# Windowed attention on one core: the values product per head in quarters of the array, and the outputs turned and sent through DRAM

## Chip, cores and metric

One core of a Trainium2 chip (trn2) runs the whole program in one launch. The metric is the time on the device in microseconds, the median of the runs; lower is better. TensorE is called PE in the rows, its weight loads PEld, VectorE DVE, ScalarE ACT, GpSimd POOL, and SyncE, which issues the DMAs, SP.

## What is computed

A macaron block over a tensor of 8 sequences x 512 tokens x 128 features: a mixture of experts, a Mamba layer, the mixture again, a second kind of mixture (top 1 of 8 experts plus a shared one), windowed attention, and that second mixture again, each added to its input. The change touches the attention alone:

```python
H, WIN, d, C = 16, 64, 8, 64              # 16 heads of 8 features
qkv = (x @ Wqkv.T + bqkv).reshape(B, S, 3, H, d).transpose(2, 0, 3, 1, 4)
...
scores = einsum('bhncd,bhnld->bhncl', qc, kb) / sqrt(d)
band = (j >= c) & (j < c + WIN)           # each query sees 64 keys around it
attn = softmax(where(band, scores, -inf))
o = einsum('bhncl,bhnld->bhncd', attn, vb).reshape(B, H, S, d)
return o.transpose(0, 2, 1, 3).reshape(B, S, D) @ Wout.T + bout
```

## The kernel before

**Units.** The attention works in 64 units. Sequence `s` has 4 groups of 4 heads, and each group two halves; unit `u` is `where(u)`: sequence `u // 8`, group `u % 8 // 2`, half `u % 2`. A unit holds 8 blocks of 32 queries; a block has its 4 heads x 32 queries on the 128 partitions and the 96 keys around it along the row. Each engine runs its own written-out loop over steps `t`, with `k = t % 8`, and semaphores tie them.

**One step of TensorE** (`pe`): the scores of unit t + 2 (`scores`, L1424, 8 matmuls of 128 x 96), the transposes of unit t (`turn`, L1450), the values product of unit t - 1 (`weigh`, L1469), and the fold of unit t - 2 (`gather`, L1491). Between them `PLACES` sets pieces of the next sequence's projections (T, q, k, v) and the output projection (op) of the last one: T at k = 0, q and k at k = 1, op at k = 2, v at k = 3; a piece of place 0 stands before the transposes, one of place 2 after the product.

**The values product** multiplies the turned probabilities of all 4 heads (96 keys x 128 rows) with 32 columns of values and 32 columns of ones, from the tile `vb`. So each row gets the values of all 4 heads of the group, of which only its own 8 columns are wanted, and its sum of probabilities. `normalize` on VectorE (L1476, L1480) divides, `keep_own` on GpSimd (L1362) multiplies with the mask `own` that leaves each head its columns, and `gather` multiplies with `fold`, four identities of 32 on top of each other. That adds the heads up, turns them, and puts them on the partitions of their group in the bank `BZ`, a quarter of the array per group. When all 8 units of a sequence are there, ScalarE copies the bank to `oT` (L1404), TensorE projects it (L1397) and VectorE adds it to `x` (L1409).

**Others.** VectorE: `mask` (scale and band, L1433), `find_max` (L1438), `set_keys` (rounds the keys of a group, L1282). GpSimd: `less_max` (subtracts the row maximum, L1355), `norm_root`, `bias_out`. ScalarE: `exps` (L1442), `copy_p` (L1457), `set_queries` (L1272, four casts of 32x512 that lay the queries of a group on a block diagonal). VectorE writes the keys and ScalarE the queries of group `t // 2 + 2` at the end of each even step t; they serve the units t + 4 and t + 5. SyncE stores the projected queries and keys to DRAM and loads them in strips per group, and does the same with the values.

**Waits.** An engine works off its own instructions in order; a wait holds all that stands behind it. `scores` of the first half of a group waits for both casts:

```python
if half == 0 and c == 0:
    eng.wait_ge(q_set.sem, q_set.at(n))
    eng.wait_ge(k_set.sem, k_set.at(n))
```

Of the kernel before, what the change touches and what calls it, by code (L numbers as in the profile page):

```python
# [7 lines left out]
F32 = mybir.dt.float32  # L8
# [176 lines left out]
def ffn0_up(nc, S, sb, w, cleared):  # L185
# [4 lines left out]
    W["raw_ld"] = [S.dma(f"f0_raw{r}_loaded", 2) for r in range(4)]  # L190
# [728 lines left out]
def front(nc, S, C, bank, lasting, xin, a, f0, K, w1, sorted_rows):  # L919
# [13 lines left out]
    with ExitStack() as ctx, ExitStack() as scan_ctx:  # L933
# [45 lines left out]
        raw_ld, split = [S.dma(f"k_raw{r}_loaded", (E + 1) * NU // 2) for r in range(4)], K["split"]  # L979
# [92 lines left out]
def attention(nc, S, C, bank, K, a, host):  # L1072
# [9 lines left out]
    RQ = 3  # L1082
    NG = NSEQ * HG
    scale = float(1.0 / np.sqrt(np.float32(HD)))
    with ExitStack() as ctx:
# [12 lines left out]
        band, own, fold = sb("band", [P, KW]), sb("own", [P, GD]), sb("fold", [P, QB])  # L1098
# [5 lines left out]
        v_rows = nc.dram_tensor("v_rows", [NSEQ * SEQ, D], F32, kind="Internal").ap()  # L1104

# [3 lines left out]
        tri = S.count("a_masks", 1, ("band", "own", "fold") + tuple(f"{n}{r}" for n in ("ge", "le", "own", "fold") for r in range(HG)))  # L1109
# [7 lines left out]
        q_set, k_set = S.count("a_queries_set", NG), S.count("a_keys_set", NG)  # L1117
        v_in = [S.dma(f"a_values{p}_in", NSEQ // 2, ("low", "mid", "high")) for p in range(2)]
        bz_zero = S.count("a_bz_zeroed")
        sc_done, sm_done, max_done, sub_done = S.count("a_scores_done", NU * 2), S.count("a_masked", NU * 2), S.count("a_max_done", NU), S.count("a_less_max", NU)  # L1120
        exp_done, turned, pT_done = S.count("a_exp_done", NU), S.count("a_p_turned", NU * 2), S.count("a_p_copied", NU * 2)
        pv_done, on_done, own_done = S.count("a_pv_done", NU * 2), S.count("a_out_dve", NU, ("rc", "on")), S.count("a_own_kept", NU)
        ot_done = S.count("a_fold_done", NU)
        oc_done, op_done, r_done, ob_done = S.count("a_oT_copied", NSEQ), S.count("a_proj_done", NSEQ), S.count("a_row_done", NSEQ), S.count("a_bias_added", NSEQ)
# [27 lines left out]
        def set_masks(eng):  # L1152
            eng.memset(band[:], 0.0).then_inc(tri.sem)
            eng.memset(own[:], 0.0).then_inc(tri.sem)
            eng.memset(fold[:], 0.0).then_inc(tri.sem)
            quarter = [slice(32 * r, 32 * r + 32) for r in range(HG)]
            for r, p in enumerate(quarter):
                eng.wait_ge(tri.sem, tri.at(0, f"ge{r - 1}" if r else "fold"))
                eng.affine_select(out=band[p, :], in_=band[p, :], compare_op=ALU.is_ge, fill=-1e30, base=0, pattern=[[1, KW]], channel_multiplier=-1).then_inc(tri.sem)
# [3 lines left out]
            for r, p in enumerate(quarter):  # L1163
                eng.wait_ge(tri.sem, tri.at(0, f"own{r - 1}" if r else "le3"))
                eng.memset(own[p, HD * r:HD * r + HD], 1.0).then_inc(tri.sem)
            for r, p in enumerate(quarter):
                eng.wait_ge(tri.sem, tri.at(0, f"fold{r - 1}" if r else "own3"))
                eng.affine_select(out=fold[p, :], in_=fold[p, :], compare_op=ALU.not_equal, fill=1.0, base=0, pattern=[[-1, QB]], channel_multiplier=1).then_inc(tri.sem)
            eng.wait_ge(tri.sem, tri.at(0, "fold3"))
# [83 lines left out]
        def strips(eng, s, g):  # L1253
# [4 lines left out]
            if n >= 2:  # L1258
                eng.wait_ge(q_set.sem, q_set.at(n - 2))
                eng.wait_ge(k_set.sem, k_set.at(n - 2))  # L1260
# [3 lines left out]
        def set_queries(eng, n, heads=range(HG)):  # L1264
# [64 lines left out]
        o1, oT = two("o1", [P, UB, GD]), sb("oT", [P, SEQ])  # L1329

        def sync(eng):
            for s in range(NSEQ):
                if s >= 1:
                    store_queries(eng, s)
                    store_keys(eng, s)
                    strips(eng, s, 0)
                    strips(eng, s, 1)
                    store_values(eng, s)
                eng.wait_ge(v_out.sem, v_out.at(s))
                if s <= 1:  # L1340
                    eng.wait_ge(zeroed.sem, zeroed.at(0, "vb"))
                else:
                    eng.wait_ge(pv_done.sem, pv_done.at(2 * (GU * (s - 1)) - 1))
                v, low, mid, high = vb[s % 2], slice(0, PAD), slice(PAD, PAD + QB), slice(PAD + QB, KW)
                rows = v_rows[s * SEQ:(s + 1) * SEQ, :].rearrange("(b i) d -> i b d", i=QB)
                eng.dma_start(v[low, 1:NB, :], rows[:, 0:NB - 1, :]).then_inc(v_in[s % 2].sem, 16)
                eng.dma_start(v[mid, 0:NB, :], rows).then_inc(v_in[s % 2].sem, 16)
                eng.dma_start(v[high, 0:NB - 1, :], rows[:, 1:NB, :]).then_inc(v_in[s % 2].sem, 16)
                strips(eng, s, 2)
                strips(eng, s, 3)  # L1350
# [6 lines left out]
        def keep_own(eng, u):  # L1357
            Z = o1[u % 2]
            if u == 0:
                eng.wait_ge(tri.sem, tri.at(0, "fold3"))  # L1360
            eng.wait_ge(on_done.sem, on_done.at(u, "on"))
            eng.tensor_tensor(Z[:], Z[:], own[:, None, :].to_broadcast([P, UB, GD]), ALU.mult).then_inc(own_done.sem)  # L1362

        def pool(eng):
            clear_group(eng, 1)
            for p in range(2):
# [6 lines left out]
            less_max(eng, 1)  # L1373
            for t in range(NU + 1):
                s, k = t // GU, t % GU
                if t + 2 < NU:
                    less_max(eng, t + 2)
# [902 lines left out]
```

## Time and profile before

| | |
|---|---|
| Time, median of 3 runs | 1867.86 us (1866.92 to 1868.22) |
| Profiled execution: span from first to last instruction | 1918.1 us |
| Profiled execution: a time of its own beside the span | none given; the span is 50.2 us above the median |
| Granted TensorE clock, mean | 0.971 |
| Busy: TensorE, VectorE, ScalarE, GpSimd | 1729.9, 1279.6, 1105.3, 1210.5 us |

The span is that of one execution under the profiler, and all start times and durations in the rows are from it. The time is measured without it. Busy time of an engine is the time in which it had an instruction running, so a TensorE that is busy need not be at its peak. The granted clock is in shares of 2.4 GHz; 0.50 is 1.2 GHz. A matmul on 32-bit floats appears as two records of weight load and two of matmul, one on rounded ones as one.

### The profile page before, as it was taken

How to read it: one execution, taken by the hardware profiler on the slowest of the kernel's cores; microseconds unless marked ns; L12 is line 12 of the kernel's file. 1: busy time of each engine (PE TensorE's matmuls, PEld its weight loads, DVE VectorE, ACT ScalarE, POOL GpSimd, SP SyncE). 2: the span in 40 equal slices, each digit the busy share in tenths (PEclk: the TensorE clock that was granted, in tenths of full speed). 3: DMA queues.
4: the chain of work that ended last, by engine and by line, in shares of the span. 5: the costliest groups of instructions: out<-in, count | busy, mean ns of one | idle time of the engine just before them, and what ended most of it. 6: DMA issues, size and time to landing. Idle time of an engine off the chain costs nothing. (4 is left out here: it accounts for less than half of the span.)

```text
span 1918.1 us, 35727 instructions
## 1 busy us (share of the span) xinstructions
PE 1729.9 (90%) x12089; PEld 1502.7 (78%) x12089; DVE 1279.6 (67%) x2981; ACT 1105.3 (58%) x1953; POOL 1210.5 (63%) x1201
## 2 busy tenths in 40 slices
PE   7998998999999899976779988899899999988889
PEld 6887776778878688765668867777899999877777
DVE  2358988888888987889894355334576766554333
ACT  3476766667676576756655452433677777542332
POOL 4248787787868778798985243565455555444554
PEclk9999999999999999998989999999899999989999
DMA  5023433323333233232224110113544554001113
GB/s 147 1 85 104 114 100 101 95 94 105 96 110 97 86 104 108 98 89 84 94 61 118 32 37 29 45 43 104 159 130 120 148 157 124 2 33 33 42 43 104
DMA packets 121486, 166.74 MB, mean 87 GB/s; under 512 B 14710, under 2 KB 56732, under 8 KB 121308
## 3 DMA queue, kind: packets, MB, share of 16 engines
q1 hardware_dynamic: 114268, 148.86, 25.7%
q0 software_dynamic: 7040, 15.60, 2.6%
q8 instruction: 101, 1.65, 0.4%
q14 instruction: 77, 0.63, 0.1%
HBM read 114.20 MB, written 50.20 MB: 86 GB/s over the span
## 5 line engine op out<-in xcount | busy, mean ns | idle before, releaser
L833 POOL TENSOR_TENSOR db<-du_m,bt 128x512 f32<-128x512 f32 x256 | 329.3, 1288 | 116.7 <-DVE bank L838 115.9
L838 DVE TENSOR_TENSOR_SCAN bank<-bank,db 128x512 f32<-128x512 f32 x256 | 312.6, 1221 | 18.2 <-ACT bank L823 17.7
L864 POOL TENSOR_TENSOR y_m<-y_m,ph 128x512 f32<-128x512 f32 x240 | 312.8, 1303 | 2.0 <-DVE ph L853 2.0
L823 ACT ACTIVATE bank<-dt_m,a_neg 128x512 f32<-128x512 f32 x256 | 176.3, 689 | 85.7 <-DVE ph L853 78.9
L853 DVE TENSOR_TENSOR ph<-bank,ct 128x512 f32<-128x512 f32 x240 | 165.9, 691 | 9.4 <-POOL y_m L864 1.1
L1355 POOL TENSOR_TENSOR s_a<-s_a,mx_a 128x768 f32<-128x768 f32 x64 | 94.1, 1470 | 87.1 <-DVE mx_a L1438 87.0
L1469 PE MATMUL bank<-vb_a,pT_a 96*128 96x64 f32 x1024 | 121.7, 272 | 0.0
L1469 PEld LDWEIGHTS bank<-vb_a,pT_a 96*128 96x128 f32 x1024 | 119.8, 193 | 0.0
L375 PEld LDWEIGHTS bank<-dn,hf1b 128*128 128x128 f32 x680 | 90.2, 194 | 16.1 <-DVE x_all L437 6.8
L375 PEld LDWEIGHTS bank<-dn,hf2b 128*128 128x128 f32 x680 | 90.2, 195 | 16.0 <-DVE x_all L437 8.3
L375 PEld LDWEIGHTS bank<-dn,hf0b 128*128 128x128 f32 x688 | 90.4, 193 | 12.0 <-DVE x_all L437 2.8
L375 PEld LDWEIGHTS bank<-dn,hf0a 128*128 128x128 f32 x688 | 91.6, 194 | 8.8 <-DVE x_all L437 1.2
L375 PE MATMUL bank<-dn,hf1b 128*128 128x128 f32 x680 | 91.7, 279 | 7.0 <-DVE x_all L437 5.0
L375 PE MATMUL bank<-dn,hf2b 128*128 128x128 f32 x680 | 91.8, 279 | 6.5 <-DVE x_all L437 6.1
L375 PEld LDWEIGHTS bank<-dn,hf2a 128*128 128x128 f32 x680 | 90.9, 195 | 7.6 <-DVE x_all L437 0.2
L375 PEld LDWEIGHTS bank<-dn,hf1a 128*128 128x128 f32 x680 | 89.8, 193 | 8.0 <-DVE x_all L437 0.6
L375 PE MATMUL bank<-dn,hf0b 128*128 128x128 f32 x688 | 91.9, 277 | 2.9 <-issue 1.5
L375 PE MATMUL bank<-dn,hf0a 128*128 128x128 f32 x688 | 91.8, 277 | 0.7 <-DVE x_all L437 0.7
L375 PE MATMUL bank<-dn,hf2a 128*128 128x128 f32 x680 | 91.5, 279 | 0.0
L375 PE MATMUL bank<-dn,hf1a 128*128 128x128 f32 x680 | 90.4, 276 | 0.1
L1457 ACT COPY pT_a<-bank 96x512 f32<-96x512 f32 x128 | 67.8, 580 | 32.2 <-PE bank L1450 32.2
L123 PE MATMUL bank<-xT_hi0b,up_hi 128*128 128x512 f32 x128 | 70.3, 549 | 17.5 <-ACT hf2b L406 9.3
(480 smaller groups left out, 4877.1 us busy)
## 6 DMA issues: line engine op xcount, KB each, us to landing
bt<-bc_rows SPq DMA_DIRECT2D x128, 256.0 KB, 3.4
ct<-bc_rows SPq DMA_DIRECT2D x128, 256.0 KB, 3.4
sorted<-zero_row SPq DMA_DIRECT2D x64, 288.0 KB, 4.0
k_strips_a<-k_rows SPq DMA_DIRECT2D x32, 256.0 KB, 3.0
q_strips_a<-q_rows SPq DMA_DIRECT2D x32, 256.0 KB, 4.0
q_rows<-q_hi_a SPq DMA_DIRECT2D x16, 256.0 KB, 3.0
q_rows<-q_lo_a SPq DMA_DIRECT2D x16, 256.0 KB, 3.3
k_rows<-k_hi_a SPq DMA_DIRECT2D x16, 256.0 KB, 3.2
```

Source lines behind the costliest of these rows:

```text
L123: eng.matmul(out, ahi, bhi, start=True, stop=False)
L375: x = eng.matmul(Y.psum[:, t], hf[r][:, t], W["dn"][:, e, c, :], start=c == 0 and k == 0, stop=c == HC - 1 and k == NT - 1, skip_group_che ...
L823: eng.activation(DH[J % 2][:], dt[s % 2][:, j % NH, :], ACT.Exp, scale=a_neg[:, j % NH, j // NH:j // NH + 1]).then_inc(da_done.sem)
L833: eng.tensor_tensor(db[J % RD][:], du[s % 2][:, j % NH, :], bt[N % RB][:], ALU.mult).then_inc(db_done.sem)
L838: eng.tensor_tensor_scan(DH[J % 2][:], DH[J % 2][:], db[J % RD][:], 0.0, ALU.mult, ALU.add).then_inc(hs_done.sem)
L853: eng.tensor_tensor(out, DH[J % 2][:], ct[N % RB][:], ALU.mult).then_inc(ph_done.sem)
L864: eng.tensor_tensor(y[s % 2][:, j % NH, :], y[s % 2][:, j % NH, :], ph[J % RP][:], ALU.add).then_inc(ys_done.sem)
L1355: eng.tensor_tensor(X[:], X[:], M[:, :, None].to_broadcast([P, UB, KW]), ALU.subtract).then_inc(sub_done.sem)
L1457: eng.copy(pT[u % 2][:, c * BB:(c + 1) * BB, :].rearrange("p b q -> p (b q)"), BT[c][0:KW, :]).then_inc(pT_done.sem)
L1469: x = eng.matmul(BO[:, at:at + 2 * GD], pT[u % 2][:, c * BB + j, :], vb[s % 2][:, b:NB + 1:NB - b, g * GD:(g + 1) * GD], start=True, stop= ...
```

## The change

`weigh` does a product of its own for each head: 32 columns of the turned probabilities stand in the quarter of the array that writes the head's 32 partitions, and 8 columns of its own values and 8 of ones move through. So the mask `own`, `keep_own`, `fold` and `gather` go. `normalize` writes 64 elements per partition instead of 256, in an order by feature and block. `turn_out` turns the whole unit with one transpose, ScalarE copies it from the bank (`copy_out`), SyncE stores it by columns in `o_rows` in DRAM (`store_out`), in runs of 32 floats, and loads the sequence as `oT` (`load_out`) for the output projection, which moves to k = 5.

With that come: scores and all before the exponential run 3 units ahead instead of 2 (`AHEAD`); two of the four query casts of each group (`set_queries` with heads 2 and 3) go to GpSimd, behind `less_max(t + 3)`, with a semaphore `q_set2` of their own that `scores` also waits for; the DMAs of SyncE have a new order; the norm of the finished sequence moves from k = 4 and 7 to k = 6, 7 and 0; before the last projection stand 20 filling matmuls instead of 4. The casts of keys and queries stay at the end of even steps.

```diff
+    AHEAD, RZ = 3, 4
+        o_rows = nc.dram_tensor("o_rows", [NSEQ, 2, HEADS, HD, UB, QB], F32, kind="Internal").ap()
...
-        def set_queries(eng, n, heads=range(HG)):
+        def set_queries(eng, copy, n, heads):
...
-                x = eng.copy(qd[n % RQ][p, :, r, :], q_strips[n % 2][p, :].rearrange("p (b q) -> p b q", q=QB))
-            if HG - 1 in heads:
-                x.then_inc(q_set.sem)
+                dst, src = qd[n % RQ][p, :, r, :], q_strips[n % 2][p, :].rearrange("p (b q) -> p b q", q=QB)
+                x = copy(dst, src)
+            x.then_inc(q_set.sem if 0 in heads else q_set2.sem)
...
+        def store_out(eng, u):
+            s, g, half = where(u)
+            eng.wait_ge(zc_done.sem, zc_done.at(u))
+            eng.dma_start(o_rows[s, half, g * HG:(g + 1) * HG, :, :, :].rearrange("r d b q -> (d b) r q"), zt[u % RZ][:]).then_inc(o_out[u % RZ].sem, 16)
+
+        def load_out(eng, s):
+            if s >= 1:
+                eng.wait_ge(op_done.sem, op_done.at(s - 1))
+            for r in range(RZ):
+                eng.wait_ge(o_out[r].sem, o_out[r].at((s + 1) * GU // RZ - 1))
+            eng.dma_start(oT[:], o_rows[s].rearrange("f h d b q -> (h d) f (b q)")).then_inc(oT_ld.sem, 16)
...
         def pool(eng):
             clear_group(eng, 1)
+            set_queries(eng, eng.tensor_copy, 1, (2, 3))
+            eng.wait_ge(q_set2.sem, q_set2.at(1))
...
-                if t + 2 < NU:
-                    less_max(eng, t + 2)
-                if t >= 1:
-                    keep_own(eng, t - 1)
+                if t + AHEAD < NU:
+                    less_max(eng, t + AHEAD)
+                if t % 2 == 0 and t + 4 < 2 * NG:
+                    eng.wait_ge(sub_done.sem, sub_done.at(t + AHEAD))
+                    set_queries(eng, eng.tensor_copy, t // 2 + 2, (2, 3))
+                    eng.wait_ge(q_set2.sem, q_set2.at(t // 2 + 2))
...
                 eng.wait_ge(q_set.sem, q_set.at(n))
+                eng.wait_ge(q_set2.sem, q_set2.at(n))
                 eng.wait_ge(k_set.sem, k_set.at(n))
...
-                b, at = half * UB + c * BB + j, (c * BB + j) * 2 * GD
-                x = eng.matmul(BO[:, at:at + 2 * GD], pT[u % 2][:, c * BB + j, :], vb[s % 2][:, b:NB + 1:NB - b, g * GD:(g + 1) * GD], start=True, stop=True)
+                b, at = half * UB + c * BB + j, (c * BB + j) * 2 * HD
+                for r in range(HG):
+                    p, h = slice(32 * r, 32 * r + 32), g * HG + r
+                    x = eng.matmul(BO[p, at:at + 2 * HD], pT[u % 2][:, c * BB + j, p], vb[s % 2][:, b:NB + 1:NB - b, h * HD:(h + 1) * HD], start=True, stop=True)
...
-        def gather(eng, u):
...
+        def turn_out(eng, u):
+            if u >= 1:
+                eng.wait_ge(zc_done.sem, zc_done.at(u - 1))
+            eng.wait_ge(on_done.sem, on_done.at(u, "on"))
+            eng.transpose(BZ[0:HD * UB, 0:P], o1[u % 2][:].rearrange("p d b -> p (d b)"), C["ident"][:]).then_inc(ot_done.sem)
+
+        def copy_out(eng, u):
+            if u >= RZ:
+                eng.wait_ge(o_out[u % RZ].sem, o_out[u % RZ].at(u // RZ - 1))
+            eng.wait_ge(ot_done.sem, ot_done.at(u))
+            eng.copy(zt[u % RZ][:], BZ[0:HD * UB, 0:P]).then_inc(zc_done.sem)
 
         def pe(eng):
-            for u in range(2):
+            for u in range(AHEAD):
...
-                if t + 2 < NU:
-                    scores(eng, t + 2, 0)
-                    scores(eng, t + 2, 1)
+                if t + AHEAD < NU:
+                    scores(eng, t + AHEAD, 0)
+                    scores(eng, t + AHEAD, 1)
...
+                    if t >= 2 and place == 2:
+                        turn_out(eng, t - 2)
                     if 1 <= t <= NU and place == 2:
                         weigh(eng, t - 1, 0)
                         weigh(eng, t - 1, 1)
...
-                if t >= 2:
-                    gather(eng, t - 2)
...
-            warm(eng, BT[0], K["up_hi"][0], 4)
+            warm(eng, BT[0], K["up_hi"][0], 20)
             project_pe(eng, NSEQ - 1)
...
                 if t % 2 == 0 and t + 4 < 2 * NG:
-                    set_queries(eng, t // 2 + 2)
+                    set_queries(eng, eng.copy, t // 2 + 2, (0, 1))
```

## Rows read from the trace of the kernel before

**Rows 1.** Page: busy us (share), instructions of TensorE.

```profile
PE 1729.9 (90%) x12089; PEld 1502.7 (78%) x12089; DVE 1279.6 (67%) x2981; ACT 1105.3 (58%) x1953; POOL 1210.5 (63%) x1201
```

**Rows 2.** Stretches: PE, PEld, DVE, ACT, POOL busy us (count), clock, DMA, GB/s.

```profile
1468.00:1506.00 38.00, 37.60 (x402) 35.38 (x401) 26.23 (x62) 27.73 (x48) 21.22 (x23) 1.00 0.48 137
```

**Rows 3.** Timeline, one step: start us, us, engine, line, instructions.

```profile
1470.98 0.97 PEld L1424 LDWEIGHTS bank<-kT_a,qd_a 128*128 128x128 f32 x8
...
1471.77 1.01 DVE L1433 SCALAR_TENSOR_TENSOR s_a<-bank,band_a 128x384 f32<-128x384 f32 x2
...
1471.90 0.83 PEld L1450 LDWEIGHTS bank<-ident,s_a 128*96 128x96 f32 x8
...
1472.71 1.87 PEld L1469 LDWEIGHTS bank<-vb_a,pT_a 96*128 96x128 f32 x16
...
1473.85 1.47 POOL L1355 TENSOR_TENSOR s_a<-s_a,mx_a 128x768 f32<-128x768 f32 x1 [1.41 <-DVE mx_a L1438]
...
1474.64 0.58 PEld L1491 LDWEIGHTS bank<-fold_a,o_a 128*32 128x32 f32 x16
...
1475.26 0.97 PEld L1424 LDWEIGHTS bank<-kT_a,qd_a 128*128 128x128 f32 x8
```

**Rows 4.** Timeline, T in two sequences, and the output projection.

```profile
1437.24 0.64 PE L114 MATMUL bank<-ident,xn_a 128*128 128x128 f32 x4
...
1448.62 1.16 PE L1397 MATMUL bank<-w_o_a,oT_a 128*128 128x128 f32 x8 [0.40 <-ACT oT_a L1404]
...
1476.19 0.64 PE L114 MATMUL bank<-ident,xn_a 128*128 128x128 f32 x4
```

**Rows 5.** Groups by shape, weight loads: busy us, mean ns, idle before.

```profile
L1491 PEld LDWEIGHTS bank<-fold_a,o_a 128*32 128x32 f32 x1024 | 37.2, 113 | 8.7 <-issue 4.5 <-POOL o_a L1362 0.4
```

**Rows 6.** Timeline, gate product of the first stage; the first two up to 126.03.

```profile
125.90 0.16 PEld L273 LDWEIGHTS bank<-xTa,wg 128*32 128x32 f32 x8
125.90 0.32 PE L273 MATMUL bank<-xTa,wg 128*32 128x128 f32 x4
...
125.90 0.43 PE L273 MATMUL bank<-xTa,wg 128*32 128x128 f32 x8
126.26 0.19 PEld L123 LDWEIGHTS bank<-xT_hi1a,up_hi 128*128 128x128 f32 x1 [0.20 <-issue]
```

**Rows 7.** Groups by shape, GpSimd: busy us, mean ns, idle before.

```profile
L1025 POOL CAST k_up_hi<-hf0a 128x512 fp32r<-128x512 f32 x5 | 3.1, 611 | 0.0
...
L217 POOL TENSOR_TENSOR b<-xnb,b 32x512 fp32r<-32x512 f32 x1 | 1.3, 1259 | 0.1
```

**Rows 8.** Timeline, key product and lower half; statistics and the next mask.

```profile
1445.50 1.08 PE L1218 MATMUL bank<-xT_a,w_k_a 128*128 128x512 f32 x2
...
1447.48 0.75 DVE L1248 SCALAR_TENSOR_TENSOR k_lo_a<-bank,b_cols_a,k_hi_a 128x512 fp32r<-128x512 f32 x1 [1.04 <-ACT k_hi_a L1239]
...
1466.84 0.86 DVE L74 BATCH_NORM_STATS2 stats_a<-x_all 128x6 f32<-128x128 f32 x4
...
1468.04 0.99 DVE L1433 SCALAR_TENSOR_TENSOR s_a<-bank,band_a 128x384 f32<-128x384 f32 x2
```

**Rows 9.** DMA issues: count, KB each, median us from issue to landing.

```profile
q_strips_a<-q_rows SPq DMA_DIRECT2D x32, 256.0 KB, 4.0
...
q_rows<-q_lo_a SPq DMA_DIRECT2D x16, 256.0 KB, 3.3
```

**Rows 10.** Timeline, end of the stage.

```profile
1670.69 1.05 PE L1397 MATMUL bank<-w_o_a,oT_a 128*128 128x128 f32 x8
...
1671.78 0.69 DVE L1409 TENSOR_TENSOR x_all<-x_all,bank 128x512 f32<-128x512 f32 x1 [3.07 <-PE bank L1397]
```

**Rows 11.** Stretches of 12 us: TensorE busy us (count), clock, DMA, GB/s.

```profile
300.00:312.00 12.00, 7.69 (x36) 0.86 0.31 85
...
540.00:552.00 12.00, 9.40 (x54) 1.00 0.20 68
...
1356.00:1368.00 12.00, 11.28 (x47) 0.50 0.53 151
```

More of the change, by code:

```diff
@@ L978, in front @@
         W["raw"], W["b2_raw"] = F["spent"], F["rows"]
-        raw_ld, split = [S.dma(f"k_raw{r}_loaded", (E + 1) * NU // 2) for r in range(4)], K["split"]
+        raw_ld, split = [S.dma(f"raw{r}_loaded", (E + 1) * NU // 2) for r in range(4)], K["split"]
         def load(eng, s):
@@ L1097, in attention @@
         q_hi, q_lo, k_hi, k_lo = (sb(n, [P, SEQ], F32R) for n in ("q_hi", "q_lo", "k_hi", "k_lo"))
-        band, own, fold = sb("band", [P, KW]), sb("own", [P, GD]), sb("fold", [P, QB])
+        band = sb("band", [P, KW])
         v_tok = xn
@@ L1108, in attention @@
         small, mats = S.dma("a_biases_loaded", 1), S.dma("a_weights_loaded", 6)
-        tri = S.count("a_masks", 1, ("band", "own", "fold") + tuple(f"{n}{r}" for n in ("ge", "le", "own", "fold") for r in range(HG)))
+        tri = S.count("a_masks", 1, ("band",) + tuple(f"{n}{r}" for n in ("ge", "le") for r in range(HG)))
         bias_p, bias_d = S.count("a_bias_pe", 1, ("cols", "all")), S.count("a_bias_dve", 1, ("cols", "all"))
@@ L1162, in set_masks @@
                 eng.affine_select(out=band[p, :], in_=band[p, :], compare_op=ALU.is_ge, fill=-1e30, base=WIN - 1, pattern=[[-1, KW]], channel_multiplier=1).then_inc(tri.sem)
[L1163 to L1169, printed above, removed]
+            eng.wait_ge(tri.sem, tri.at(0, "le3"))
         def biases_pe(eng):
@@ L1350, in sync @@
-                strips(eng, s, 3)
+                    store_out(eng, u - 2)
+                if more:
+                    store_queries(eng, s + 1)
+                if s >= 1:
+                    store_out(eng, u - 1)
+                if more:
+                    store_keys(eng, s + 1)
+                store_out(eng, u)
+                if s >= 1:
+                    load_out(eng, s - 1)
+                if more:
+                    strips(eng, s + 1, 0)
+                    strips(eng, s + 1, 1)
@@ new lines, in sync @@
+                store_out(eng, u + 1)
+                if more:
+                    store_values(eng, s + 1)
+                    load_values(eng, s + 1)
+                store_out(eng, u + 2)
+                if more:
+                    strips(eng, s + 1, 2)
+                store_out(eng, u + 3)
+                store_out(eng, u + 4)
+                if more:
+                    strips(eng, s + 1, 3)
+                store_out(eng, u + 5)
+            store_out(eng, NU - 2)
+            store_out(eng, NU - 1)
@@ L1479, in normalize @@
             eng.wait_ge(on_done.sem, on_done.at(u, "rc"))
-            eng.tensor_tensor(Z[:], O[:, :, 0:GD], R[:, :, None].to_broadcast([P, UB, GD]), ALU.mult).then_inc(on_done.sem)
-        def gather(eng, u):
-            s, g, half = where(u)
-            if u == 0:
-                eng.wait_ge(bz_zero.sem, bz_zero.at(0))
-            if u % GU == 0 and s >= 1:
-                eng.wait_ge(oc_done.sem, oc_done.at(s - 1))
-            eng.wait_ge(own_done.sem, own_done.at(u))
-            for j in range(UB):
-                b = half * UB + j
-                x = eng.matmul(BZ[32 * g:32 * g + 32, b * QB:(b + 1) * QB], o1[u % 2][:, j, :], fold[:], start=True, stop=True)
-            x.then_inc(ot_done.sem)
+            eng.tensor_tensor(Z[:].rearrange("p d b -> p b d"), O[:, :, 0:HD], R[:, :, None].to_broadcast([P, UB, HD]), ALU.mult).then_inc(on_done.sem)
+        def turn_out(eng, u):
[8 more added lines that the diff above has]
+            eng.copy(zt[u % RZ][:], BZ[0:HD * UB, 0:P]).then_inc(zc_done.sem)
         def pe(eng):
-            for u in range(2):
+            for u in range(AHEAD):
                 for c in range(2):
@@ L1527, in act @@
             norm_out(eng, 1)
-            set_queries(eng, 1)
+            set_queries(eng, eng.copy, 1, (0, 1))
             exps(eng, 0)
@@ L1540, in act @@
                         copy_p(eng, t, 1)
+                    if place == 2 and t >= 2:
+                        copy_out(eng, t - 2)
                     for name in PLACES[k][place]:
-                        if name == "op" and s >= 1:
-                            project_act(eng, s - 1)
                         if name != "op" and s + 1 < NSEQ:
```

107 lines of the change are left out of this document (48 added, 59 removed).

## The prediction

> **What bounds the kernel now.** I read the page first: TensorE is the busiest engine of the run [rows 1]. The change touches one stage, the attention, which the timeline shows up to 1671.78 + 0.69 = 1672.5 us [rows 10]. The table of stretches says that inside it TensorE has no idle time worth a name (37.6 of 38 us) while VectorE, ScalarE and GpSimd are busy 26, 28 and 21 of 38, and that its granted clock is full [rows 2]. So the stage is paid by TensorE's program, and I read one step of that program in the timeline by the starts of its weight loads [rows 3]: scores 0.92 us (1470.98 to 1471.90), transposes 0.81, values product 1.93, fold 0.62, in all 4.28. Like points of neighbouring sequences lie 38.95 apart (1437.24 and 1476.19) [rows 4]; less 8 x 4.28 = 34.24 that leaves 4.71 for the projections: the four transposes of T, 0.12 each, 0.48 together; 0.40 a wait for the ScalarE copy of the output [rows 4]; the other 3.83 is work that stands in the odd steps 1, 3 and 5 after the change.
>
> **The values product.** One 96x128 load with 64 moving columns becomes four 96x32 loads with 16 columns: 64 records per unit instead of 16. The trace has two cases of 32-column loads. In the fold all 16 go to one quarter of the array: (0.58 - 0.11)/15 = 31 ns apart [rows 3, 5]. In the gate product of the first stage the quarters alternate: its eight loads, each 0.11 long, lie within 0.16; four of its 128-column matmuls are started within 0.32, ends included, all eight within 0.43, and the next work starts 0.36 after the first load [rows 6]. Loads of 31 ns in turn would need 0.25 for eight, so quarters overlap. The new code alternates quarters. Bounds for 64 records: all in turn, 64 x 31 ns + 0.20 to leave = 2.2 us; four at a time, 16 x 31 ns + 0.20 to leave (0.36 less the 0.16) + 0.14 to enter (1.93 less 16 times the (1.87 - 0.19)/15 = 0.112 between loads of the old product) = 0.84. I take 0.84, because the gate product is the case with the same pattern. The fold (0.62) goes. One transpose of 64 columns comes, taken as 0.25 with its own change of shape; its lower bound is 0.10, a transpose's share of 0.81. A step becomes 0.92 + 0.81 + 0.25 + 0.84 = 2.82 us. Alone, that would save 1.46 us in each of 64 steps, over 90 us.
>
> **Where it goes.** Scores run three units ahead now, but keys and queries for unit t + 4 are still written at the end of the even step t. Before, TensorE came to that unit in step t + 2, now in step t + 1: a whole step of slack is gone. Half of the query casts also move to GpSimd, behind its subtraction for unit t + 3, whose input are the scores that TensorE makes at the start of the same step t. From the start of an even step, scores, mask, maximum and subtraction end after 1473.85 + 1.47 - 1470.98 = 4.34 us [rows 3]. Then come two 32x512 casts on GpSimd. The nearest row is its 128x512 cast, 0.61; 32 partitions don't shorten it, since an operation of two inputs takes 1259 ns over 32x512 and 1.47 us over 128x768 [rows 3, 7]. 4.34 + 1.22 + 0.10 for two handovers = 5.66 us before the next step may start, and all that TensorE has queued stands behind that wait. By the same reading ScalarE's half and VectorE's key cast end near 4.3, earlier, so GpSimd decides. Even step 5.66, odd step 2.82: a pair takes 8.48 where it took 8.56. TensorE's saving is turned into a wait.
>
> Two even steps are longer still. Step 2: the lower half of the keys ends 1447.48 + 0.75 - 1445.50 = 2.73 us after the start of the key product, which takes 1.0 and is the last work of step 1; masks then start 1.75 into step 2 instead of 0.79 (1471.77), +0.96 [rows 3, 8]. Step 6: the statistics of the next sequence hold VectorE 1.20 (1466.84 to 1468.04), after a normalization that ends 0.7 to 0.8 into the step; masks start at 1.96, +1.17 [rows 8]. Before, neither was waited for, since all of it lay beside TensorE's work.
>
> **The sum.** A sequence: odd steps 4 x 2.82 + 3.83 = 15.11; even 4 x 5.66 + 0.96 + 1.17 = 24.77 (T lies in a wait); 39.88 against 38.95, +0.93. Seven of them, the seventh without statistics: +5.3. The last sequence ran from 1437.24 - 0.93 + 5 x 38.95 = 1631.1 to 1672.5, 41.4 us. After: two even steps 11.3, steps 1, 3 and 4 8.5, three without scores 2.2 each by ScalarE (an estimate: 27.73 us in 8 steps [rows 2] less casts and projections) with 2.7 for the output projection and the next stage's first normalization, then 1.5: 30.6. Then the new way out: copy 0.3, a store to DRAM and its load, with 3.3 and 4.0 us to landing as nearest rows [rows 9], the projection 1.05, the addition 0.69 [rows 10] and handovers 0.2: 9.5. Together 40.1, -1.3. At the start GpSimd has two casts ahead of its first subtraction (1.2) and the queries of group 2 behind its fourth; I put +3, between 0.5 and 4.5. Off the path: GpSimd's own-head multiplication goes, VectorE's normalization shrinks to a quarter, and 64 small stores and 8 loads come to DMA engines that are at 0.48 [rows 2]; the first of them that is awaited has over two steps to land. In all +5.3 - 1.3 + 3 = +7.
>
> **The clock.** TensorE would be busy 8 x 2.82 + 4.31 = 26.9 of 39.9 us, 0.67, with waits of 2.8 and, in steps 2 and 6, near 4 us. A stretch of 12 us with such a share (7.69 us busy) shows 0.86 granted, which is part of it at 1.2 GHz, and the start of this very stage, after a pause, 0.50 for 12 us; but 9.40 of 12 shows 1.00 [rows 11]. At 0.86 the lower level holds 28% of the time. The work that matters (odd steps and the scores of even ones, 15.1 + 3.7 = 18.8 us a sequence) loses half of that, 2.6 us, 20 over the stage. Some of it falls into waits; I take two thirds, +13.
>
> +7 + 13 = +20. The sum is of differences in the profiled execution, whose span of 1918.1 us is 50.2 above the median run of 1867.86; I add it to the median unscaled: 1888 us.
>
> **Rivals.** (a) The forecast, chance 0.45: quarters overlap, GpSimd's queries set the even steps. Its own range is 1870 to 1903.
>
> (b) The quarters overlap little, or such short instructions can't be supplied so fast; the product takes 1.5 us (halfway between the bounds) to 2.2. The odd steps, some 35 with those of the last sequence, grow by 0.66 to 1.36: +23 to +48 on the +7, with few falls of the clock, so 1898 to 1923. For it: no row shows a long stream of so short instructions. Against it: rows 6. Chance 0.25.
>
> The Trainium skill, TensorE: Matmul & The Clock Gate, section "Wait — 56ns, not 53.3ns?", states a floor of about 25 ns between the starts of two matmuls, however few their columns. By that rule, an estimate, the product would take 64 x 25 ns + 0.34 = 1.9 us and the kernel about 1912, a case of (b); the gate product, with four starts close together, speaks against it for alternating quarters.
>
> (c) The other side, faster or no change. One mechanism: the odd step gets short enough to pay for the wait. With a product of 0.5 (no edges) and a transpose of 0.10 a step is 2.33, and 35 x 0.49 = 17 comes off +7: 1858. The sum is zero at a step of 2.6. It decides if the clock also stays full, as in the stretch with 9.40 of 12 us busy [rows 11]. Chance 0.22.
>
> (d) The clock stays at the lower level through most of the stage, as at its start [rows 11]: 35 odd steps nearly double, +60 us or more. Chance 0.08.
>
> The range leaves out (d) and the end of (c): 1862 to 1925. Within 0.2% (3.7 us, about what a measurement of this kernel can tell from no change) counts as the same. From (c) faster 0.14, same 0.08; with a little of (a): same 0.10, slower 0.76.
>
> **What would show it.** In the timeline after, the 64 records of a product within 1 us, or over 1.3 for (b). Scores that wait for GpSimd's cast of the queries, some 30 times, 2.8 us each and near 4 in steps 2 and 6; if that wait is named for VectorE's keys, or missing, my chain is wrong. A period of 39.9 us per sequence plus what the clock takes, with a granted clock of 0.8 to 0.9; 1.00 would take 13 us off. After the last copy out, 9 us to the last addition. The forecast fails if the scores don't wait, if GpSimd's casts of 32 partitions are much shorter than 0.61, or if the product isn't near one of its bounds.

## The result, and the profile after

The changed kernel takes 1942.43 us, the median of 4 runs (1941.02 to 1944.51), beside 1867.58 for the kernel before (1866.92 to 1868.22, 4 runs): ratio 1.040, 95% interval 1.0385 to 1.0414. The forecast was 1888 and its range 1862 to 1925. So it is slower, as forecast, but by 75 us, not 20. The profiled execution has a span of 1942.8 us and a time of its own of 1944.51.

The page of the kernel after, the slices of the granted clock (each is a fortieth of the span, 48.6 us, and the digit is in tenths):

```profile
PEclk9999999999999899998899999997677778789999
```

The attention stage runs from 1333.45 to 1721.49 us, 388.0 us, where it took 318.4 before. In none of the nine slices that it touches is the clock full. The stretch with all but its ends says it in one row, and stretches of 12 us inside it show between 0.50 and 0.86, in no order by the busy time of TensorE (columns: PE, PEld, DVE, ACT, POOL busy us, clock, DMA, GB/s):

```profile
1343.00:1711.00 368.00, 275.03 (x5258) 241.99 (x5260) 216.99 (x488) 187.82 (x363) 156.91 (x167) 0.75 0.40 114
...
1380.00:1392.00 12.00, 9.84 (x165) 8.83 (x164) 5.72 (x13) 6.95 (x15) 5.42 (x6) 0.50 0.17 51
...
1440.00:1452.00 12.00, 10.74 (x185) 8.75 (x189) 6.77 (x15) 7.39 (x14) 5.72 (x6) 0.82 0.16 43
1452.00:1464.00 12.00, 7.93 (x167) 7.58 (x167) 7.34 (x14) 4.74 (x10) 4.24 (x4) 0.72 0.83 252
```

TensorE is busy 275 of 368 us, where it had been busy all the time [rows 2]. A granted clock of 0.75 is half of the time at 1.2 GHz. Its waits, by the list of waits from 1380 to 1650 us (in total, times, longest):

```profile
PEld bank L1451 <- issue: 64.8, 29, 4.2
PE bank L1451 <- POOL qd_a L1268: 63.7, 19, 4.1
...
PEld bank L1451 <- ACT qd_a L1268: 7.3, 5, 1.6
PE bank L1451 <- DVE kT_a L1277: 3.8, 3, 1.3
```

L1451 are the scores, L1268 the casts of the queries. That is the wait that was forecast, on the engine that was forecast. Within a sequence it is 4.07 us behind step 2, 3.05 behind step 4 and 4.05 behind step 6 (the scores at 1456.80, 1468.41 and 1481.81); near 4, 2.8 and near 4 were forecast. Behind step 0 it is 1.3 us, for VectorE's keys. One of them, and the steps around it, in the timeline:

```profile
1451.95 0.78 PE L1498 MATMUL bank<-vb_a,pT_a 96*32 96x16 f32 x64
...
1453.83 1.47 POOL L1390 TENSOR_TENSOR s_a<-s_a,mx_a 128x768 f32<-128x768 f32 x1 [2.74 <-DVE mx_a L1465]
...
1454.11 1.47 DVE L1277 CAST kT_a<-k_strips_a 128x512 fp32r<-128x512 f32 x1
1455.36 1.34 POOL L1268 CAST qd_a<-q_strips_a 32x512 fp32r<-32x512 f32 x2
...
1456.80 1.91 PE L1451 MATMUL bank<-kT_a,qd_a 128*128 128x96 f32 x8 [4.07 <-POOL qd_a L1268]
...
1458.43 1.83 PEld L1216 LDWEIGHTS bank<-w_v_a,xT_a 128*128 128x128 f32 x8
...
1462.59 1.09 PE L1451 MATMUL bank<-kT_a,qd_a 128*128 128x96 f32 x8
...
1464.62 0.64 PEld L1498 LDWEIGHTS bank<-vb_a,pT_a 96*32 96x32 f32 x64 [0.20 <-issue]
1464.62 0.74 PE L1498 MATMUL bank<-vb_a,pT_a 96*32 96x16 f32 x64
```

Read it from the wait. TensorE ends the product of an even step at 1452.7 and waits until 1456.8. What follows runs at half speed: the scores take 1.91 us where the next ones, at 1462.59, take 1.09, and the eight loads of v 1.83 against 0.97 at full clock (fill18, below). When the clock is back, the next even step has begun, and with it the next wait. The 64 records of the product end within 0.74 us. The period, by the starts of T (1390.82, 1440.22, 1488.31, 1537.22, 1587.18, 1633.23), is 46.1 to 50.0 us, 48.5 on the mean; it was 38.95 [rows 4], and 39.9 plus the clock was forecast.

The end of the stage:

```profile
1714.12 0.26 ACT L1521 COPY zt_a<-bank 64x128 f32<-64x128 f32 x1 [1.79 <-PE bank L1515]
1714.41 0.57 SPq L1330 DMA_DIRECT2D o_rows<-zt_a  x1
1716.88 0.38 SPq L1337 DMA_DIRECT2D oT_a<-o_rows  x1
1719.60 0.97 PEld L1429 LDWEIGHTS bank<-w_o_a,oT_a 128*128 128x128 f32 x8 [1.42 <-DMA oT_a<-o_rows]
...
1720.80 0.69 DVE L1435 TENSOR_TENSOR x_all<-x_all,bank 128x512 f32<-128x512 f32 x1 [6.71 <-PE bank L1429]
```

From the last copy to the last addition it is 7.4 us, where 9.5 was forecast from larger transfers [rows 9].

### The profile page after: what moved, and what is told of

Its sections match the earlier page's. It is cut to its first block and busy times, and to the rows that moved or that the text cites. A ratio compares the mean times of both kernels' runs of the same rounds, so it can differ in the third digit from the quotient of the medians.

```text
span 1942.8 us, 40247 instructions
## 1 busy us (share of the span) xinstructions
PE 1692.8 (87%) x14217; PEld 1452.9 (75%) x14217; DVE 1292.6 (67%) x2980; ACT 1076.6 (55%) x1947; POOL 1200.5 (62%) x1189
## 5 line engine op out<-in xcount | busy, mean ns | idle before, releaser
L1451 PE MATMUL bank<-kT_a,qd_a 128*128 128x96 f32 x512 | 97.5, 348 | 95.2 <-POOL qd_a L1268 88.7
L1451 PEld LDWEIGHTS bank<-kT_a,qd_a 128*128 128x128 f32 x512 | 87.8, 257 | 102.3 <-issue 91.1
L1460 DVE SCALAR_TENSOR_TENSOR s_a<-bank,band_a 128x384 f32<-128x384 f32 x128 | 68.1, 552 | 66.4 <-PE bank L1451 65.9
L1477 PE MATMUL bank<-ident,s_a 128*96 128x128 f32 x512 | 96.3, 352 | 0.0
```

What stands on the lines that cost most here:

```text
L1451: x = eng.matmul(BS[c][:, j * KW:(j + 1) * KW], qd[n % RQ][:, b, :, :].rearrange("p r q -> p (r q)"), kT[n % RQ][:, b * QB:b * QB + KW], s ...
L1460: eng.scalar_tensor_tensor(sc[u % 4][:, c * BB:(c + 1) * BB, :], BS[c][:, 0:BB * KW].rearrange("p (b k) -> p b k", k=KW), scale, band[:, N ...
L1477: x = eng.transpose(BT[c][0:KW, j * P:(j + 1) * P], sc[u % 4][:, c * BB + j, :], C["ident"][:])
```

## The experiments

The experiments ran on three chips (7, 14 and 12 on record), and on each of them the kernel before takes 1919 to 1921 us and not 1868. So each is told by its ratio to the kernel before on the same chip and by the length of its attention stage, from the first scores to the last addition of the output projection. Expectations in microseconds are meant for the first chip; a ratio times 1867.6 stands beside them. Two kernels make this reading safe: the kernel before and the changed one once more.

**The kernel before, again (before_again).** No edit.

> The kernel before, unedited, for a second profile: its runs took 1867.86 us, the profiled execution had a span of 1918.1, and the kernels of the first four experiments ran beside runs of it that took 1918.98. What I expect: the attention stage and its period of 38.95 us are the same in either kind of execution, within 0.5%, and the 50 us lie in the stages ahead of it and behind it.

Measured: a time of 1918.46 us, span 1916.7. The stage takes 316.1 us (318.4 in the first profile; the difference lies in its first sequence), the period is 38.95, the clock 1.00:

```profile
1367.00:1663.00 296.00, 293.26 (x3117) 277.24 (x3117) 203.62 (x488) 212.50 (x365) 165.03 (x168) 1.00 0.42 125
```

**The changed kernel, again (after_again).** No edit.

> The changed kernel, unedited, on the same chip as the others of this set: a fair partner for them. Expected: a ratio of 1.035 to 1.045 to the kernel before, as in the first comparison, with the attention stage at 380 to 392 us.

Measured: 1993.68 us, ratio 1.0383 (1.0351 to 1.0415), the stage 388.8 us, the clock in it again 0.75. Against the first profile of the changed kernel, 21.3 us lie ahead of the stage (start at 1354.70 instead of 1333.45) and 26.7 behind it (248.0 instead of 221.3), and 0.8 in it. So the chips differ outside the attention, as far as these profiles show, and the profile of before in this document, with its span 50 us over the median, is one of the slower kind. I take it that the stage's length can be compared between all profiles here, though chips 7 and 12 have no profile of an unedited kernel: 388.8 less 316.1 is 72.7 us, which is the whole of the loss.

**Filling the wait (fill12, fill18).** The edit to the changed kernel, here with 18 matmuls that compute nothing that is used, and with 12 in `fill12`:

```diff
                 if t + AHEAD < NU:
+                    if (t + AHEAD) % 2 == 0:
+                        eng.wait_ge(sm_done.sem, sm_done.at(2 * (t + AHEAD - 1)))
+                        for _ in range(18):
+                            eng.matmul(BS[0][:, P:], K["up_hi"][0][:, 0, 0:P], K["up_hi"][0][:, 0, P:], start=True, stop=True)
                     scores(eng, t + AHEAD, 0)
```

> The changed kernel with 12 idle matmuls of 384 columns put into TensorE's program at the start of each odd step, right ahead of the scores that wait for the queries. They take the place of the wait (about 1.9 us at full clock of a wait of 4) and compute nothing that is used. Theory 1 (the clock is the mis-sized term: TensorE falls to 1.2 GHz in its waits, and the scores behind them then lengthen the very chain that it waits for): the granted clock in the stage rises above 0.95, the scores of odd steps take 0.97 us instead of 1.8, the period of a sequence falls from 49 us to 40 or 41, and the kernel to 1870 to 1895 us. Theory 2 (the chain on VectorE and GpSimd is by itself longer than I worked out, and the low clock only falls into waits): the clock rises too, but the period stays at 47 us or more and the kernel above 1925 us. Theory 3 (the DMAs or the way through DRAM hold the stage up): no change, 1940.

> The changed kernel with 18 idle matmuls instead of the 12 of the first experiment, at the same place (start of each odd step, ahead of the waiting scores): about 2.9 us at full clock, the wait that I had worked out is 2.84. With 12 the stage fell from 388 to 339 us and the mean clock in it was 0.93, so a part of the low clock was left. Theory 1 (the chain at full clock is as I worked it out, 5.66 us an even step): clock above 0.98, periods of 39.5 to 41 us, the stage 325 to 335 us. Theory 2 (the chain at full clock is longer than 5.66): clock above 0.98 but periods of 41.5 us or more, the stage 338 or more.

Measured: with 12, ratio 1.0099 (1.006 to 1.0139), 1886 us on the first chip, stage 338.7 us, clock 0.93, periods of 40.0 to 46.0. With 18, ratio 1.0042 (1.0025 to 1.0059), stage 324.8 us, clock 1.00, periods of 39.9 to 40.4. The stretch of the stage with 18, and its timeline around one even step:

```profile
1366.00:1671.00 305.00, 295.25 (x5791) 269.09 (x5789) 217.95 (x488) 182.80 (x362) 155.70 (x167) 1.00 0.49 137
```

```profile
1504.91 0.97 PEld L1451 LDWEIGHTS bank<-kT_a,qd_a 128*128 128x128 f32 x8
...
1507.61 3.07 PEld L1533 LDWEIGHTS bank<-k_up_hi 128*128 128x128 f32 x18
...
1507.76 1.47 POOL L1390 TENSOR_TENSOR s_a<-s_a,mx_a 128x768 f32<-128x768 f32 x1 [2.10 <-DMA q_strips_a<-q_rows]
...
1509.29 1.34 POOL L1268 CAST qd_a<-q_strips_a 32x512 fp32r<-32x512 f32 x2
...
1510.70 1.00 PEld L1451 LDWEIGHTS bank<-kT_a,qd_a 128*128 128x128 f32 x8
```

With 18 it is theory 1 (the stage 0.2 us under its range). With 12 the time is that of theory 1, but the clock and the periods miss what it named: the filling was too short. The run with 18 is the forecast without its clock: from the scores at 1504.91 the subtraction ends after 4.32 us (4.34 forecast), the casts after 5.72, the next scores start after 5.79 (5.66). TensorE's own work in the step is 2.70 (2.82). The stage is 8.7 us over that of the kernel before, and +7 was forecast. The filling takes TensorE's idle time and shortens nothing in the chain (scores, masks, maximum, subtraction, casts, next scores), yet the stage is 64.0 us shorter with it (388.8 to 324.8): that is the price of the low clock. Most of the waiting scores start 0.07 us behind the end of GpSimd's casts. In one step of each sequence they start only when the filling ends, 0.2 to 0.6 us late, about 2.4 us in all, so at full clock the chain may cost up to that much less than 8.7 us and the clock as much more than 64.0.

**Two units ahead (ahead2).** In the changed kernel alone:

```diff
-    AHEAD, RZ = 3, 4
+    AHEAD, RZ = 2, 4
```

> The changed kernel with the scores two units ahead instead of three, all else as it is (product per head, outputs through DRAM, half of the query casts on GpSimd). Theory 1 (the lost step of slack makes the waits, and the waits make the low clock): the scores no longer wait 4 us in each odd step, the granted clock is above 0.97, a sequence takes 26 to 30 us (8 steps of 2.7 and 4.3 for the projections, or what ScalarE needs), and the kernel takes 1775 to 1815 us, faster than the kernel before. Theory 2 (GpSimd's casts behind its subtraction, or small instructions and stores, cost as much with two units ahead): a period of 38 us or more and a kernel of 1870 or more.

Measured: ratio 0.9789 (0.9756 to 0.9822), 1828 us on the first chip, stage 272.6 us, clock 0.93, periods of 32.0 to 34.1. Theory 1 has the direction, but its time (1775 to 1815), clock and period all missed. The waits of 4 us are gone, and the kernel is faster than the kernel before. But a sequence takes 33 us and not 26 to 30. What I had not expected stands in the list of waits from 1380 to 1620 us:

```profile
DVE kT_a L1277 <- DMA q_strips_a<-q_rows: 23.9, 7, 3.9
ACT qd_a L1268 <- DMA q_strips_a<-q_rows: 22.7, 7, 3.8
PE bank L1451 <- POOL qd_a L1268: 19.1, 14, 2.9
POOL qd_a L1268 <- DMA q_strips_a<-q_rows: 17.2, 7, 3.1
```

Once a sequence all three engines wait over 2 us for the strips of the next sequence's first group, which make a round trip through DRAM. With steps of 2.7 us instead of 4.3 the same trip spans more steps than it is given. The change also puts 64 small stores and 8 loads into SyncE's queue, and no run separates the two causes.

**The casts first (first).** In the changed kernel, three units ahead, on GpSimd (VectorE and ScalarE alike):

```diff
+                if t % 2 == 0 and t + 4 < 2 * NG:
+                    eng.wait_ge(sub_done.sem, sub_done.at(t + AHEAD - 1))
...
+                    set_queries(eng, eng.tensor_copy, t // 2 + 2, (2, 3))
+                    eng.wait_ge(q_set2.sem, q_set2.at(t // 2 + 2))
                 if t + AHEAD < NU:
                     less_max(eng, t + AHEAD)
-                if t % 2 == 0 and t + 4 < 2 * NG:
-                    eng.wait_ge(sub_done.sem, sub_done.at(t + AHEAD))
-                    set_queries(eng, eng.tensor_copy, t // 2 + 2, (2, 3))
-                    eng.wait_ge(q_set2.sem, q_set2.at(t // 2 + 2))
```

> The changed kernel, three units ahead, with the casts of keys and queries moved from the end of the even step to its start on all three engines (GpSimd casts ahead of its subtraction, VectorE ahead of the masks, ScalarE ahead of the exponential). They need nothing of that step, only the strips and a free buffer. Theory 1 (it is the order behind less_max of the same step that makes the wait, not three units ahead as such): the waits for the queries go, clock above 0.97, kernel 1775 to 1815 us. Theory 2 (the strips come too late for that, or the masks and exponentials pushed back by the casts now hold TensorE): 1850 us or more.

Measured: ratio 1.0058 (1.0036 to 1.008), stage 322.0 us, clock 0.80. The time of theory 1 did not come, but its cause is there. In most steps the wait is gone, and 67 us with it. But the casts now want the strips a step earlier still, and stand in front of everything else of their engines:

```profile
1455.40 1.47 POOL L1390 TENSOR_TENSOR s_a<-s_a,mx_a 128x768 f32<-128x768 f32 x1 [0.82 <-DVE mx_a L1471]
1462.79 1.49 POOL L1268 CAST qd_a<-q_strips_a 32x512 fp32r<-32x512 f32 x2 [5.92 <-DMA q_strips_a<-q_rows]
```

GpSimd stands for 5.9 us, TensorE behind it for 5.6, and then runs at the lower level. Over seven sequences VectorE waits 42.6 us in this way, against 1.0 us in the changed kernel, where its casts come late enough. This is theory 2, a second bound behind the first.

**All query casts on ScalarE (all_act).** In the changed kernel, three units ahead:

```diff
                 if t % 2 == 0 and t + 4 < 2 * NG:
                     set_queries(eng, eng.copy, t // 2 + 2, (0, 1))
+                    set_queries(eng, eng.copy, t // 2 + 2, (2, 3))
```

and the two casts of GpSimd's loop taken out.

> The changed kernel, three units ahead, with all four query casts back on ScalarE at the end of the even step, and none on GpSimd after the start. Theory 1 (the missing step of slack decides, the engine of the casts only shifts it): ScalarE's four casts end about when GpSimd's two did, some 5.5 us into the even step, and the kernel stays between 1925 and 1960 us. Theory 2 (the move to GpSimd alone is what costs): the even steps shorten by 1.2 us or more each, 28 of them and their low clock, and the kernel takes 1900 us or less.

Measured: ratio 1.0283 (1.0252 to 1.0314), stage 377.3 us, clock 0.75. By the ratio it would be 1921 us on the first chip, between the two theories and nearer to the first: GpSimd's place costs some 11 us of the 73. It was not what cost most.

**Three ahead alone (before_ahead3), and filled (ahead3_fill).** The kernel before with `t + 3` in place of `t + 2` in the loops of TensorE, VectorE and GpSimd, and a third unit ahead of the loops; nothing else of the change:

```diff
-                if t + 2 < NU:
-                    scores(eng, t + 2, 0)
-                    scores(eng, t + 2, 1)
+                if t + 3 < NU:
+                    scores(eng, t + 3, 0)
+                    scores(eng, t + 3, 1)
```

> The kernel before with the scores three units ahead instead of two, and nothing else of the change (old product, mask, fold, all queries cast on ScalarE). Theory 1 (three ahead takes away the step of slack, but it is the shorter step of TensorE that uncovers the chain): ScalarE's casts end about when TensorE's even step of 4.3 us does, waits of 0 to 1.2 us a pair, clock 1.00 in the stage, 0 to +35 us. Theory 2 (three ahead alone makes the waits of 3 to 4 us, whatever the product): a granted clock of 0.8 in the stage and +60 us or more.

> The kernel before with three units ahead (which took 6% more than the kernel before, the stage 425 us, with waits of 0.7 to 1.5 us for ScalarE's queries and a clock of 0.77), and 6 idle matmuls of 384 columns, about 1 us, ahead of the scores that wait. Theory 1 (short waits bring the clock down, and TensorE, which is busy nearly all the time, then pays for it in full): clock above 0.97, the stage 330 to 355 us, ratio 1.01 to 1.025. Theory 2 (the clock falls for another cause, the waits are a consequence): no change, ratio 1.05 or more.

Measured: without filling, ratio 1.0603 (1.0542 to 1.0664), stage 424.8 us, clock 0.77: slower than the whole change. With 6 idle matmuls, ratio 1.0174 (1.0149 to 1.0198), stage 352.1 us, clock 0.99, periods of 43.2. The first expectation missed: neither of its theories names waits so short with a loss so large. The waits are short, as theory 1 had it, and the clock falls, as theory 2 had it. List of waits from 1380 to 1760 us, and stretches of 12 us, without filling:

```profile
PEld bank L1425 <- ACT qd_a L1272: 23.0, 25, 1.5
PE bank L1425 <- ACT qd_a L1272: 20.5, 25, 1.4
```

```profile
1410.00:1422.00 12.00, 10.79 (x103) 9.15 (x103) 7.55 (x14) 7.03 (x13) 5.79 (x6) 1.00 0.42 128
...
1518.00:1530.00 12.00, 10.79 (x81) 10.41 (x80) 6.46 (x12) 6.20 (x12) 4.29 (x4) 0.75 0.67 207
1530.00:1542.00 12.00, 11.78 (x79) 11.31 (x78) 4.20 (x12) 4.93 (x8) 2.99 (x3) 0.50 0.30 70
1542.00:1554.00 12.00, 12.00 (x69) 11.68 (x70) 6.54 (x24) 3.30 (x6) 6.07 (x10) 0.50 0.15 44
1554.00:1566.00 12.00, 11.78 (x79) 11.31 (x78) 3.74 (x9) 6.42 (x12) 3.48 (x4) 0.50 0.15 45
1566.00:1578.00 12.00, 11.78 (x61) 10.40 (x61) 4.99 (x9) 4.95 (x8) 2.45 (x3) 0.50 0.00 0
1578.00:1590.00 12.00, 10.79 (x105) 9.57 (x104) 5.69 (x12) 7.78 (x13) 5.74 (x5) 0.97 0.57 176
```

A kernel that TensorE bounds pays for each microsecond at the lower level in full, and here one fall lasted 48 us. The filled kernel parts the loss of 108.7 us: 36.0 are the chain at full clock (352.1 less 316.1), 72.7 the clock. Here TensorE no longer waits for the queries at all, and nearly every filling ends about 0.1 us after the casts, so about 3 of the 36 may be the filling's own. So three units ahead costs 33 to 36 us at full clock with the old product, where TensorE works 4.28 us a step; all the rest of the change (product, outputs, GpSimd's casts) gives 27.3 back (352.1 to 324.8, the two filled kernels).

**What is left with two ahead (odd_first, ahead2_act, ahead2_fill).** Three edits to `ahead2`. The casts at the start of the odd step:

```diff
+                if t % 2 == 1 and t + 3 < 2 * NG:
+                    set_keys(eng, t // 2 + 2)
                 if t + AHEAD < NU:
                     mask(eng, t + AHEAD, 0)
...
-                if t % 2 == 0 and t + 4 < 2 * NG:
-                    set_keys(eng, t // 2 + 2)
```

(the queries on ScalarE and GpSimd likewise); all query casts on ScalarE, as in `all_act`; and 12 idle matmuls at the start of step 6 alone (`if k == 6:` in the edit of `fill12`).

> The changed kernel with the scores two units ahead, and the casts of keys and queries moved on all three engines from the end of the even step to the start of the odd step behind it: they are wanted one step later, and stand ahead of that step's subtraction, masks and exponential. Two units ahead alone gave a period of 33.7 us with waits for GpSimd's queries (19.9 us in the stage), for the masks (7.0) and for the load of the outputs (3.3). Theory 1 (what is left in it is the same wait for queries that stand too late on GpSimd): the waits for queries go, the period falls to 28 to 31 us, ratio 0.955 to 0.97. Theory 2 (what is left is the supply of strips, which come late because SyncE's queue now holds 64 small stores and 8 loads ahead of them): a wait for the strips takes its place once a sequence, the period stays at 32 to 35 us, ratio 0.975 to 0.985.

> The changed kernel with two units ahead and all four query casts on ScalarE, none on GpSimd: of the change only the product per head, the turning and the way through DRAM are left, with the new order of SyncE. Two units ahead with half of the casts on GpSimd gave a ratio of 0.979 and a stage of 272.6 us. Theory 1 (ScalarE, busy 212.6 of 298 us before, becomes the long engine with a step of 2.8 us): the stage 272 to 285 us, no better than with GpSimd's casts. Theory 2 (GpSimd's casts behind its subtraction are the wait that was left): the stage 255 to 268 us.

> The changed kernel with two units ahead, and 12 idle matmuls at the start of step 6 of each sequence alone, where the scores of the next sequence's first group wait 2 us because their strips come late from DRAM. Theory 1 (that one wait brings the clock down for the steps behind it): granted clock of 0.97 or more in the stage instead of 0.93, the stage 260 to 268 us instead of 272.6, ratio 0.972 to 0.977. Theory 2 (what the clock gives back is eaten by waits for the strips and the chain): stage and ratio unchanged within 0.3%.

Measured: `odd_first` 0.9754 (0.9723 to 0.9784), stage 275.3 us, clock 0.88; `ahead2_act` 0.9856 (0.9833 to 0.9879), stage 289.0, clock 0.84; `ahead2_fill` 0.9777 (0.9751 to 0.9802), stage 273.8, clock 0.96. The first and the last can't be told from `ahead2`. With `odd_first` the waits for the strips stay (26.1 us on VectorE, 26.9 in `ahead2`) and the ratio is in the range of its theory 2. Its theory 1 is out: TensorE's waits for GpSimd's queries stay too (20.2 us in the stage, 19.9 in `ahead2`), though the casts now stand ahead of the subtraction. With `ahead2_act` the stage is longer by 16 us, more than either theory said: with steps so short GpSimd's help is worth its place. With `ahead2_fill` the clock rises and the time does not follow, theory 2. The wait of TensorE for the strips is filled, but the masks behind the late keys are waited for in its place (list of waits from 1380 to 1620 us):

```profile
DVE kT_a L1277 <- DMA q_strips_a<-q_rows: 21.7, 7, 3.8
...
PEld bank L1533 <- DVE s_a L1460: 9.7, 6, 2.6
...
PE bank L1451 <- DVE s_a L1460: 8.5, 7, 1.6
PE bank L1451 <- POOL qd_a L1268: 5.0, 9, 1.0
```

L1533 are here the filling matmuls. Version `ahead2`, one constant away from the change, beats both kernels by 2.1% and 5.7% (0.9789, and 0.9789 / 1.0383 = 0.943).

## Why the prediction was right in sign and wrong in size

**The values product: right, and a little better.** Of the bounds 2.2 and 0.84 us the lower was taken. The 64 loads take 0.64 us, and from the first of them to the next work it is 0.67 (1506.94 to 1507.61 in fill18), 10 ns a load; less the 0.11 that the last load takes, the starts of the loads are (0.64 - 0.11)/63 = 8 ns apart. Rival (b), 1.5 to 2.2 us, is out, and so is the estimate of 1.9 us: the rule of the Trainium skill, TensorE: Matmul & The Clock Gate, section "Wait — 56ns, not 53.3ns?", of 25 ns between two starts does not hold here for quarters in turn. A step is 2.70 us instead of 2.82.

**Where it goes: right.** The scores of odd steps wait for GpSimd's queries; the even step at full clock is 5.79 us (5.66 forecast), the period 40.2 (39.88), the stage +8.7 us (+7). The casts are 0.65 us each on the mean (0.61). VectorE's key cast was put near 4.3 us into the step and ends at 4.6 (1508.21 + 1.30 - 1504.91 in fill18), still before GpSimd's at 5.72. That the sum for full clock comes so near has some luck in it. In fill18 against before_again, the start with the first sequence costs 6.1 us (3.9 forecast), the five sequences behind it 6.5 (4.7), and the rest gives 3.9 back (1.5 forecast).

**The end: off by 2 us.** 7.4 us from the copy to the addition, 9.5 forecast. The store of 32 KB was 2.5 us from its start to the load, the load 2.7 us to the projection.

**The clock: the step that failed.** The forecast had "At 0.86 the lower level holds 28% of the time ... half of that, 2.6 us, 20 over the stage. Some of it falls into waits; I take two thirds, +13." Measured: 64.0 us (after_again less fill18) in place of the 13, a clock of 0.75 and so half of the time at the lower level. Three things in that step were wrong.

First, the row. A stretch of 12 us with TensorE busy for 7.69 showed 0.86 [rows 11]; here a stretch with 7.93 us busy shows 0.72. The busy time does not say what clock is granted. In three ahead alone TensorE was busy 10.79 us in three stretches of 12, and they show 1.00, 0.75 and 0.97.

Second, the feedback. Busy time and waits were taken from the chain at full clock and the clock put on top once. But behind most waits of 3 us or more the engine starts at the lower level (scores of 1.8 to 1.9 us; behind a few, as at 1603.76, 1.06), and what it starts with is the scores on which the masks, the subtraction and so the next casts hang: 0.8 us late in the row above. And the odd step behind it takes longer, so that more of the period is slow.

Third, the discount. "Some of it falls into waits" allowed a third. The row of v in the timeline shows the order: the low clock comes behind the wait, over the scores, v and transposes of the odd step, which nothing hides.

The measured 48.5 us a period on the mean less 40.2 is 8.3 us, three times the 2.6 that were written down, before the discount. Rival (d), "odd steps nearly double, +60 us or more", was the right mechanism with 0.08, and it was left out of the range. The numbers to give it more were there: the start of this very stage shows 0.50 for 12 us behind a pause, with 11.28 us busy [rows 11].

**Rival (c)**, a step short enough to pay for the wait, needed 2.6 us; with 2.70 it failed by a little at full clock, and at the clock granted it was far off. That the whole change is carried down by one of its parts is shown: with two units ahead instead of three the same product, outputs and casts give 0.979. The forecast named that slack ("a whole step of slack is gone") and had no term for what the rest is worth with it.

**What stays open.** With two ahead a sequence takes 33 us, 7 more than TensorE's 25.9 (8 steps of 2.70 and 4.3 for the projections). I estimate from the waits that about 2 are the late strips and under 1 the load of the outputs. About 2 are the low clock: TensorE is busy for 236.6 us in the stage, and in fill18, less its 30 fillings of 3.07 us, for 221, over 8 sequences. The rest are short waits for queries and masks. Sending the projections of the next sequence off a step or two earlier would test it; that wasn't tried.

## What to carry to other kernels

A wait on TensorE can cost its own length and then what stands behind it at 1.2 GHz; cost both, and cost the second on the path, as a feedback, where the work behind the wait feeds the wait itself. If a stage is to have regular waits of 3 to 4 us, take half of it at the lower level as a real case, not as a tail. Test the suspicion at once with idle matmuls in the wait: they part the clock (here 64 us) from the chain (8.7 us) in one run. Look whether the filling or the awaited work ends last in each wait: here it was 12 matmuls too few and 18 a little too many.

When an engine's step gets shorter, look at every distance that is counted in steps: the round trip of the strips through DRAM was far enough apart at 4.3 us a step and is not at 2.7. And when work is moved a unit ahead, look at what is written for it: the casts lost a step of slack by that alone, at 4.3 us a step as well. Undo such distances one by one before the main idea is given up.

## What the runs showed of the hardware that was not expected

- TensorE stayed at 1.2 GHz for 48 us (1530 to 1578 in three ahead alone) though it was busy for 11.78 us or more in each stretch of 12, and stretches with less busy time in the same kernel show 1.00. The waits ahead of that fall were of 0.8 us (as at 1523.85). The same waits stand in the stretches at 1.00 (1392.34, 1411.72), so they don't say when the clock falls.
- Matmuls on a quarter of the array with 16 columns, the quarters in turn, follow each other in 10 ns or less (64 loads in 0.64 us); those of the fold, all on one quarter, were 31 ns apart [rows 3, 5]. The fold also has 128 rows and 32 columns, and no run changes the quarter alone.
- A cast of 128x512 on VectorE that began while GpSimd's subtraction ran ended 0.28 to 0.29 us after that subtraction, however long it had still to run: so 23 of the 32 casts in the changed kernel, with 0.84 to 1.54 us each, and 30 of 32 in fill18. The row of 1454.11 is one: it ends at 1455.58, the subtraction at 1455.30. The other 9 took 0.41 to 0.52. So it looks as if the cast waits for the subtraction to end. The mean over 32 was 516 ns before, 1120 in the changed kernel, and 518 in the kernel with the casts first, where only 3 begin within it. Masks and maximums, which take 0.5 and 0.95 us, showed no such thing in the rows read. No experiment isolated it.
- Chips differ: the same program ran in 1868 us on the first and in 1919 to 1921 on three others, the changed one in 1942 and in 1994. For the changed kernel the difference lies in other stages (21.3 us ahead of the attention and 26.7 behind it); the attention stage agrees within 0.8 us, and the ratios (1.040 and 1.038) do.
